# A two-layer convolution kernel: the filtered right-neighbour product in group one too, pair rounds between border batches, four stores from GpSimd

## The chip, the core and the metric

The kernel runs on one core of a Trainium2 chip. The core has TensorE (matmuls, into the accumulators `acc` in PSUM), VectorE, ScalarE, GpSimd and SyncE, each with its own instruction stream; they wait for each other by semaphores. Sixteen DMA engines move data to and from memory. The metric is the device time of one execution in microseconds (us), the median of several runs.

## The reference

Eight images of 32 channels and 64 x 64 pixels in float32. Two residual layers follow each other; `_gn` normalises each image and channel over its pixels.

```python
def _L0_conv_ref(x, w3, b3, w5, b5, wr, br):
    y3 = conv(x, w3) + b3            # 3 x 3, SAME
    y5 = conv(x, w5) + b5            # 5 x 5, SAME
    P = jnp.pad(y3, ((0, 0), (0, 0), (1, 1), (1, 1)))
    shifts = [P[:, :, 2 - sw:2 - sw + H, 2 - sh:2 - sh + W] for sh in range(3) for sw in range(3)]
    stacked = jnp.stack([y5] + shifts, axis=2)
    return jnp.einsum('bcghw,cg->bchw', stacked, wr[:, :, 0, 0]) + br[None, :, None, None]

def _L1_conv_ref(x, filters):        # filters: 32 x 32 x 10 x 10
    spot = _extract_patches(x, 3, 1, 1)                  # the 9 pixels around each pixel
    spot = jnp.concatenate([ones, spot], axis=-1)        # 1 and the 9 pixels
    feat = (spot[..., :, None] * spot[..., None, :]).reshape(spot.shape[:-1] + (M * M,))
    return jnp.einsum('bcyxf,ocf->boyx', feat, filters.reshape(O, C, M * M))

x = x + _L0_conv_ref(_gn(x), ...)
x = x + _L1_conv_ref(_gn(x), filters)
```

The second layer needs, for each channel, the pixels, their squares and the products of each pixel with its neighbours. The product of a pixel with its right neighbour is called NEXT in the kernel, the others have the numbers 7 to 17.

## The kernel before

**Tiling.** The images are worked on in two groups of four: group one (g = 0, images 0 to 3) and group two (g = 1, images 4 to 7). A group fills the 128 partitions, 32 channels by 4 images, in `raw[g]` (the input, later x after layer one) and in `plane[g]` (normalised, with borders). TensorE is used as a grid of 32 x 32 tiles: the row of the grid is the image r, the column the strip s. There are four strips of an image: s // 2 says which half of the rows, s % 2 which parity of rows. Even and odd pixel columns are summed apart, in `acc[:, 0]` and `acc[:, 1]` (j or `odd`).

**Rounds.** A filter column of three taps (`column`, L994 to L1023; layer one has the like in `column0`) is done in *pair rounds*, 8 matmuls with 64 columns of weights that serve two strips at once, and a *single round*, 16 matmuls with 32 columns of weights. Three rows of taps take two pair rounds and one single round. The order is an argument (`PS`, `SP`).

**Streams.** VectorE writes the products that TensorE reads as *streams*: a tile (`product[0..3]`, `raw0` or `raw1`, by `UNIT_HOME`) with an even and an odd half. `multiply` (L876) makes one product with 4096 elements a partition. The tiles are used in turn, so `wait_free` lets VectorE wait until TensorE has used what was there.

**Minimal filtering.** For the pixels themselves (linear) and their squares, even and odd columns are not filtered apart. VectorE makes sums and differences of neighbouring half-streams (`linear`, `of_product`: a sum, a cross, a left and a right one), and TensorE filters each with one set of three taps: `mixed_unit` for the sum and the cross, `side_unit` for left and right. The sum unit (j = 0) and the cross unit (j = 1) go to both outputs. ScalarE copies them out of `acc` (`keep_sum`, `keep_cross`), and VectorE adds them again in `mix` and `evict`. In group two the product NEXT is done in this way as well, with the shared taps `next_sum` and the sides `next left` and `next right`. In group one NEXT goes through `taps1`: two columns of taps for either parity.

**The order of the work.** It is written out by hand, engine by engine. TensorE: layer one of group one, layer one of group two, with the border batches of group one in it (`edges0`: matmuls of 64 pixels for the sides of the image), then for each group the shared units, the cross units, the sides, the products 7 to 17. The border batches of group two stand in the shared units of group one. Around them:

```python
keep_sum(0)            # ScalarE: waits for shared_done
spread(1, 0, (2,))
keep_cross(0)          # waits for the cross units
spread(1, 0, (3,))     # 4 copies
spread(1, 1, range(GROUP))   # 16 copies
```

`spread(g, odd, images)` copies layer one's result into `raw[g]`. On VectorE, `finish_x1(1)` (L817) waits for all these copies; behind it stand the statistics of group two, its normalisation, products 9 and 10, `mix(0)` and products 11 to 17:

```python
multiply(0, 7)
multiply(0, 8)
finish_x1(1)
step(statistics(1, lambda n: None, every))
normalise(3)
make_offset()
multiply(0, 9)
multiply(0, 10)
mix(0)
for u in range(11, LAST_UNIT + 1):
    multiply(0, u)
```

Layer one of group two on VectorE: `whole_and_cross(1)` (L663) needs TensorE's "step" part, then come `finish_x1(0)`, the statistics of group one's second layer, `normalise(2)` and `finish_even(1)` (L669), for which TensorE's first rounds of layer two wait.

**The end.** VectorE adds and writes the result in `evict` (L801), one image at a time. In group one SyncE stores all strips. In group two SyncE stores strips 0 and 1 and ScalarE strips 2 and 3: 16 stores of 128 KB, in rows of 256 bytes. SyncE waits for all of them.

Of the kernel before, what the change touches and what calls it, by code (L numbers as in the profile page):

```python
# [6 lines left out]
GROUP = 4  # L7
# [58 lines left out]
def n_taps(d):  # L66
# [11 lines left out]
UNIT_HOME = ({LINEAR: 1, SQUARE: 3, SQUARE_MIXED: 0, NEXT: 2, LINEAR_SIDES: "raw0", SQUARE_SIDES: 1,  # L78
              7: 3, 8: 0, 9: "raw0", 10: 1, 11: 2, 12: 3, 13: 0, 14: "raw0", 15: 1, 16: 2, 17: 3},
             {LINEAR: 0, SQUARE: "raw1", SQUARE_MIXED: 1, NEXT: 2, LINEAR_SIDES: 3, SQUARE_SIDES: 0, NEXT_SIDES: 1,  # L80
              7: "raw1", 8: 2, 9: 3, 10: 0, 11: 1, 12: "raw1", 13: 2, 14: 3, 15: 0, 16: 1, 17: "raw1"})


USED = ([LINEAR, SQUARE_MIXED, LINEAR_SIDES, SQUARE_SIDES, NEXT] + list(range(7, LAST_UNIT)),
# [3 lines left out]
MADE = (["square sum", "linear cross", "square cross", "linear left", "next", "square left", "linear right",  # L88
         "square right"] + list(range(7, LAST_UNIT + 1)),
# [9 lines left out]
def conv_kernel(nc, x, w3, b3, w5, b5, wr, br, filters, out):  # L99
# [12 lines left out]
    with ctx:  # L112
# [3 lines left out]
        def sem(name):  # L116
            return ctx.enter_context(nc.semaphore(name))
# [108 lines left out]
        stored = sem("stored")  # L226

# [76 lines left out]
        def store(eng, g, r, strips):  # L304

            for s in strips:
# [3 lines left out]
                              .rearrange("p (y x) -> p y x", x=W)).then_inc(stored, 16)  # L310
# [13 lines left out]
        def _(sp):  # L324
# [12 lines left out]
            for r in range(GROUP):  # L337
                sp.wait_ge(evicted, GROUP + r + 1)
                store(sp, 0, r, range(STRIPS))
            for r in range(GROUP):  # L340
                sp.wait_ge(evicted, 3 * GROUP + r + 1)
                store(sp, 1, r, (0, 1))
            sp.wait_ge(stored, 16 * NG * GROUP * STRIPS)

        @block.gpsimd
        def _(pool):
# [119 lines left out]
            stream_borders(raw[1]).then_inc(borders, 1)  # L466

        @block.scalar
        def _(act):
# [135 lines left out]
            for r in range(GROUP):  # L605
                act.wait_ge(evicted, 3 * GROUP + r + 1)
                store(act, 1, r, (2, 3))

        @block.vector
        def _(dve):  # L610
# [226 lines left out]
            def wait_free(g, u):  # L837

                if g == 0:
                    before = {SQUARE_SIDES: LINEAR, 8: SQUARE_MIXED, 9: LINEAR_SIDES, 10: SQUARE_SIDES, 11: NEXT,  # L840
                              12: 7, 13: 8, 14: 9, 15: 10, 16: 11, 17: 12}.get(u)
                    dve.wait_ge(borders, {3: 1, 0: 2, 1: 3, "raw0": 4, 2: 5}[UNIT_HOME[g][u]])
                elif u in (LINEAR, SQUARE_MIXED, NEXT, LINEAR_SIDES):
                    wait_used(dve, 0, {LINEAR: 13, SQUARE_MIXED: 15, NEXT: 16, LINEAR_SIDES: 17}[u])
                    before = None
                else:
                    before = {SQUARE_SIDES: LINEAR, NEXT_SIDES: SQUARE_MIXED, 8: LINEAR, 9: LINEAR_SIDES,
# [437 lines left out]
```

## Time and profile before

| | |
|---|---|
| median of 3 runs (lowest, highest) | 304.87 us (304.46, 305.16) |
| profiled execution, its own time | 305.6 us |
| its span, first to last instruction | 303.9 us |
| TensorE, weight loads, VectorE, ScalarE, GpSimd: busy share of the span | 91%, 41%, 83%, 29%, 11% |
| mean granted clock of TensorE | 0.979 |
| written to and read from memory | 4.19 and 6.40 MB |

The span is that of the profiled execution; 1.7 us of its own time lie around it. A busy share is a mean over the whole span. The timeline tells the start of a run of like instructions, its length, and in brackets how long the engine was idle before it and who released it; "issue" means that the profile shows nobody. The granted clock is 1.00 where TensorE runs at its upper level (2.4 GHz) and 0.50 at the lower (1.2 GHz). Each matmul of this kernel leaves two records and so does its weight load: 3232 matmuls, 6464 records.

### The profile page before, as it was taken

To read this page: it belongs to the slowest core of one execution; us is meant where nothing else is said; L and a number is where in the kernel's file an instruction comes from. 1 tells how busy PE (TensorE), PEld (TensorE's weight loads), DVE (VectorE), ACT (ScalarE), POOL (GpSimd) and SP (SyncE) were. 2 spreads that over 40 slices of the span, in tenths; PEclk is the share of its full clock that TensorE was granted. 3 is DMA by queue.
4 is the path that set the end of the run, shared out by engine and by line. 5 is a ranking of instruction groups with operands and counts; after the bars stand their busy time and mean duration, and the time that the engine had idled before them with its cause. 6 is when DMAs were issued, how large, how long until landed. Compare 5 with 4: busy or idle time off the path is not lost.

```text
span 303.9 us, 13566 instructions
## 1 busy us (share of the span) xinstructions
PE 276.0 (91%) x6464; PEld 125.6 (41%) x6464; DVE 251.5 (83%) x216; ACT 88.1 (29%) x135; POOL 33.0 (11%) x82
## 2 busy tenths in 40 slices
PE   0579999899999999999999999999999999999930
PEld 0124443343334434436457455333334446447310
DVE  1899899995999999599999999976999999950330
ACT  5432016949258989529000000004000000000000
POOL 7913970000110000000000000000000000000000
PEclk9999999979999999999999999999999999999985
DMA  6973000000000000000000000085000000000049
GB/s 191 382 193 82 4 3 2 2 5 2 2 2 4 4 2 2 4 2 5 2 2 4 4 2 4 2 172 111 2 2 4 2 2 4 2 4 4 2 86 190
DMA packets 19206, 11.45 MB, mean 38 GB/s; under 512 B 17744, under 2 KB 17872, under 8 KB 19024
## 3 DMA queue, kind: packets, MB, share of 16 engines
q1 hardware_dynamic: 14640, 9.06, 11.7%
q10 hardware_dynamic: 4512, 1.53, 2.2%
q8 instruction: 50, 0.82, 1.2%
q14 instruction: 4, 0.03, 0.0%
HBM read 6.40 MB, written 4.19 MB: 35 GB/s over the span
## 4 chain that ended last, share of the span: by engine, by line
PE 80%; DVE 7%; ACT 3%; issue 3%; DMA 2%; SPq 1%; DVEq 0%
PE acc L1007 63%; PE acc L1050 15%; ACT raw L507 3%; DMA raw<-in_x 2%; DVE stats L741 2%; PE acc L1101 2%; DVE plane L759 1%; DVE raw L801 1%; DVE arena L669 1%; ACT arena L497 1%; DVE scaled L637 0%; DVE norm L756 0%; SPq L314 0%; SPq L321 0%; DVE mean_var L746 0%
## 5 line engine op out<-in xcount | busy, mean ns | idle before, releaser
L1007 PE MATMUL acc<-product,weight 32*32 32x512 f32 (+1 forms) x3040 | 128.6, 605 | 0.0
L1007 PEld LDWEIGHTS acc<-product,weight 32*32 32x32 f32 (+1 forms) x3040 | 61.7, 110 | 63.8 <-issue 51.1
L879 DVE TENSOR_TENSOR product<-plane 128x4096 f32<-128x4096 f32 x19 | 83.3, 4427 | 0.1
L1007 PE MATMUL acc<-raw,weight 32*32 32x512 f32 (+1 forms) x992 | 44.3, 605 | 0.0
L1050 PE MATMUL acc<-product,middle 32*64 32x512 f32 (+1 forms) x576 | 30.6, 621 | 0.0
L1007 PEld LDWEIGHTS acc<-raw,weight 32*32 32x32 f32 (+1 forms) x992 | 20.4, 111 | 20.7 <-issue 16.2
L801 DVE TENSOR_TENSOR raw<-acc,arena 128x512 f32<-128x512 f32 x16 | 9.9, 684 | 18.9 <-issue 18.7
L741 DVE BATCH_NORM_STATS2 stats<-raw 128x6 f32<-128x512 f32 x32 | 19.7, 686 | 3.1 <-DMA raw<-in_x 3.1
L879 DVE TENSOR_TENSOR raw<-plane 128x4096 f32<-128x4096 f32 x5 | 22.2, 4433 | 0.0
L1007 PE MATMUL acc<-product,arena 32*32 32x512 f32 (+1 forms) x448 | 22.0, 606 | 0.0
L507 ACT ACTIVATE raw<-arena 32x512 f32<-32x512 f32 x32 | 21.9, 683 | 0.5
L537 ACT ACTIVATE arena<-acc 128x2048 f32<-128x2048 f32 x2 | 3.8, 1882 | 61.5 <-PE acc L1007 61.5
L507 ACT ACTIVATE raw<-product 32x512 f32<-32x512 f32 x28 | 19.2, 685 | 2.7 <-DVE product L669 2.3
L637 DVE TENSOR_TENSOR product<-plane 128x2048 f32<-128x2048 f32 (+1 forms) x8 | 18.5, 2324 | 0.0
L1050 PEld LDWEIGHTS acc<-product,middle 32*64 32x64 f32 (+1 forms) x576 | 11.0, 127 | 17.3 <-issue 17.1
L1120 PE MATMUL acc<-raw 32*64 32x512 f32 x64 | 5.7, 837 | 12.1 <-DMA raw<-in_x 11.0
L872 DVE TENSOR_TENSOR product<-product 128x2048 f32<-128x2048 f32 x6 | 13.6, 2289 | 0.6 <-PE acc L1007 0.6
L1007 PEld LDWEIGHTS acc<-product,arena 32*32 32x32 f32 (+1 forms) x448 | 7.5, 116 | 13.3 <-issue 12.5
L872 DVE TENSOR_TENSOR product<-raw 128x2048 f32<-128x2048 f32 x4 | 9.0, 2299 | 4.6 <-PE acc L1007 4.6
L860 DVE TENSOR_TENSOR product<-plane 128x2048 f32<-128x2048 f32 x5 | 11.3, 2297 | 0.0
L1050 PE MATMUL acc<-plane,weight 32*64 32x512 f32 (+1 forms) x192 | 10.4, 633 | 0.7 <-DVE plane L759 0.7
L1050 PE MATMUL acc<-product,minus_one 32*64 32x512 f32 (+1 forms) x192 | 10.8, 600 | 0.0
(121 smaller groups left out, 213.9 us busy)
## 6 DMA issues: line engine op xcount, KB each, us to landing
raw<-in_x SPq DMA_DIRECT2D x8, 512.0 KB, 8.5
out<-raw SPq DMA_DIRECT2D x24, 128.0 KB, 2.9
arena<-in_L_conv_filters SPq DMA_DIRECT2D x4, 400.0 KB, 6.9
out<-raw ACTq DMA_DIRECT2D x8, 128.0 KB, 4.6
arena<-in_L_conv_w ACTq DMA_DIRECT2D x4, 100.0 KB, 4.0
w_in<-in_L_conv_w ACTq DMA_DIRECT2D x2, 36.0 KB, 1.9
w_in<-in_L_conv_w SPq DMA_DIRECT2D x2, 36.0 KB, 2.1
b_in<-in_L_conv_b SPq DMA_DIRECT2D x2, 0.5 KB
```

The costliest lines, as they stand in the source:

```text
L507: last = nc.scalar.activation(to[:, y:y + SIDE_ROWS - 1:2, odd:odd + W - 1:2], half[32 * s:32 * s + 32, CHUNK * r:CHUNK * r + CHUNK] .rear ...
L537: nc.scalar.activation(kept_sum, part_acc(0), ACT.Copy).then_inc(shared_kept, 1)
L637: nc.vector.tensor_tensor(lines(buf, at, pitch)[:, 2:2 + H, 0:width], every_second(one), every_second(other), ALU.add if name == "total" e ...
L741: last = nc.vector.bn_stats(stats[:, n, :], raw[g][:, STAT * n:STAT * n + STAT])
L801: nc.vector.tensor_tensor(view(result, 2 * CHUNK * r + odd, (W, CHUNK // HALF_W), (2, HALF_W)), acc[:, odd, r, :].rearrange("p (y x) -> p ...
L860: nc.vector.tensor_tensor(half_stream(g, u, half), plane_half(g, one), plane_half(g, other), ALU.add if (sides, half) == (0, 0) else ALU.s ...
L872: nc.vector.tensor_tensor(half_stream(g, u, half), half_stream(g, source, *one), half_stream(g, source, *other), ALU.add if (sides, half) ...
L879: nc.vector.tensor_tensor(both_halves(g, u), plane_halves(g), plane_halves(g, PRODUCTS[k][0] * PITCH + PRODUCTS[k][1]), ALU.mult)\
L1007: return nc.tensor.matmul(acc[32 * s:32 * (s + strips), j, r, :], weights[32 * r:32 * r + 32, t:t + strips, :] .rearrange("p t c -> p (t c ...
L1050: return nc.tensor.matmul(acc[32 * s:32 * (s + strips), odd, r, :], five[32 * r:32 * r + 32, t:t + strips, :].rearrange("p t c -> p (t c)" ...
L1101: last = nc.tensor.matmul(acc[32 * s:32 * s + 32, 1, side, 0:W], weight0[32 * r:32 * r + 32, EDGE_AT + 5 * EDGE_PLACE[side] + t + 2, :], p ...
L1120: nc.tensor.matmul(acc[32 * s:32 * s + 64, 1, r, :], raw[0][32 * r:32 * r + 32, 0:64], raw[0][32 * r:32 * r + 32, 0:CHUNK], start=True, st ...
```

## The change

1. Group one computes NEXT by minimal filtering too. `next_unit` (three rounds) comes behind the square sum, ahead of the cross units, and `side_unit` does the left and the right side; the two columns of `taps1` fall away. VectorE makes NEXT as its second stream and adds `next left` and `next right`. The tiles of the streams are handed out anew, and group one's orders of pair and single rounds become those of group two; its products 7 to 17 begin with single rounds.
2. Between the two border batches of group one stand two pair rounds in the place of one single round; between those of group two four pair rounds in the place of two single ones, which go ahead of the first batch. Layer one's remaining parts of group two begin with single rounds.
3. In the 16 stores of group two strip 0 is SyncE's, strip 1 ScalarE's and strip 2 GpSimd's; strip 3 goes to ScalarE for images 0 and 2 and to SyncE for 1 and 3. GpSimd's four count on a semaphore of their own, for which SyncE waits last.

```diff
+USED = ([LINEAR, SQUARE_MIXED, LINEAR_SIDES, SQUARE_SIDES, NEXT_SIDES] + list(range(7, LAST_UNIT)),
+MADE = (["square sum", "next", "linear cross", "square cross", "linear left", "linear right", "square left",
+         "square right", "next left", "next right"] + list(range(7, LAST_UNIT + 1)),
...
+        def store_last(eng, strips, parity, done):
+
+            for r in range(GROUP):
+                eng.wait_ge(evicted, 3 * GROUP + r + 1)
+                store(eng, 1, r, strips + ((3,) if r % 2 == parity else ()), done)
...
-            for r in range(GROUP):
-                sp.wait_ge(evicted, 3 * GROUP + r + 1)
-                store(sp, 1, r, (0, 1))
-            sp.wait_ge(stored, 16 * NG * GROUP * STRIPS)
+            store_last(sp, (0,), 1, stored)
+            sp.wait_ge(stored, 16 * (NG * GROUP * STRIPS - GROUP))
+            sp.wait_ge(stored_by_pool, 16 * GROUP)
...
+            store_last(pool, (2,), None, stored_by_pool)
...
-            for r in range(GROUP):
-                act.wait_ge(evicted, 3 * GROUP + r + 1)
-                store(act, 1, r, (2, 3))
+            store_last(act, (1,), 0, stored)
...
             square_sum(0)
+            multiply(0, NEXT)
             linear_cross(0)
             square_cross(0)
             linear_left(0)
-            multiply(0, NEXT)
+            linear_right(0)
             square_left(0)
-            linear_right(0)
             square_right(0)
+            next_left(0)
+            next_right(0)
...
             edges0(0, ROW_SIDES)
-            product0(1, "total", 0, False, False, False)
+            product0(1, "total", 0, False, False, True, (-1, 0))
             edges0(0, COLUMN_SIDES)
-            product0(1, "total", 0, False, True, True).then_inc(part_done, 1)
+            product0(1, "total", 0, False, False, True, (1, 2))
+            product0(1, "total", 0, False, True, False).then_inc(part_done, 1)
             pe.wait_ge(edges_copied, 2)
-            rest0(1, PAIRS_FIRST)
+            rest0(1, SINGLES_FIRST)
...
+            def next_unit(g):
+
+                pe.wait_ge(stream_made, made(g, "next"))
+                column(0, stream_pixels(g, NEXT, 0), every_row, next_sum, False, False, PAIRS)
+                column(0, stream_pixels(g, NEXT, 0), every_row, next_sum, False, True, SINGLES)\
+                    .then_inc(shared_done, 1)
...
-                        column(0, plane_pixels(0, half), every_row, sum_taps[0][:, 0:3, :], half == 0, False, PAIRS)
+                        column(0, plane_pixels(0, half), every_row, sum_taps[0][:, 0:3, :], half == 0, False, SINGLES)
                     edges0(1, ROW_SIDES)
                     for half in (0, 1):
-                        column(0, plane_pixels(0, half), every_row, sum_taps[0][:, 0:3, :], False, False, SINGLES)
+                        column(0, plane_pixels(0, half), every_row, sum_taps[0][:, 0:3, :], False, False, PAIRS)
                     edges0(1, COLUMN_SIDES)
                     pe.wait_ge(borders, 5)
-                    mixed_unit(g, 0, "square", SP, stop=True).then_inc(shared_done, 1)
+                    mixed_unit(g, 0, "square", SP)
+                    next_unit(g)
...
-                side_unit(g, 0, "linear", SP if g else PS, start=True)
-                side_unit(g, 0, "square", PS if g else SP)
-                if g:
-                    side_unit(g, 0, "next", SP)
-                else:
-                    wait_made(g, NEXT)
-                    taps1(g, 0, NEXT, PAIRS)
-                    taps1(g, 0, NEXT, SINGLES)
+                side_unit(g, 0, "linear", SP, start=True)
+                side_unit(g, 0, "square", PS)
+                side_unit(g, 0, "next", SP)
                 pe.wait_ge(shared_kept, 2 * g + 2)
...
-                in_pairs = g == 0
+                in_pairs = False
```

TensorE at the first border place, in layer one of group two; rows of 32x64 (L1101) and 32x1 are a border batch, 64x512 are pair rounds (8 matmuls each), 32x512 single rounds (16). Before:

```order
16 L1050 MATMUL acc<-plane1,weight0 32x512 x16
17 L1101 MATMUL acc<-plane0,weight0 32x64 x40
18 L1109 MATMUL acc<-plane0,weight0 32x1 x16
19 L1050 MATMUL acc<-product3,middle0_1 32x512 x16
20 L1101 MATMUL acc<-plane0,weight0 32x64 x40
21 L1050 MATMUL acc<-product3,middle0_1 64x512 x64
22 L1050 MATMUL acc<-product3,middle0_1 32x512 x16
23 L1050 MATMUL acc<-product0,weight0 32x512 x16
```

The same place now:

```order
16 L1053 MATMUL acc<-plane1,weight0 32x512 x16
17 L1104 MATMUL acc<-plane0,weight0 32x64 x40
18 L1112 MATMUL acc<-plane0,weight0 32x1 x16
19 L1053 MATMUL acc<-product3,middle0_1 64x512 x16
20 L1104 MATMUL acc<-plane0,weight0 32x64 x40
21 L1053 MATMUL acc<-product3,middle0_1 64x512 x16
22 L1053 MATMUL acc<-product3,middle0_1 32x512 x32
23 L1053 MATMUL acc<-product3,middle0_1 64x512 x32
24 L1053 MATMUL acc<-product0,weight0 64x512 x32
```

Two pair rounds took the single round's place between the batches; behind the second batch follow two pair rounds, two single rounds and four pair rounds, where eight pair rounds and a single one ended the "step" part.

TensorE in layer two of group one, from the square sum (`product0`) to the cross units (reads of `product1` and `product0` with `arena` weights) and the first side. Before:

```order
36 L1007 MATMUL acc<-product0,arena 32x512 x16
37 L1007 MATMUL acc<-product0,arena 64x512 x16
38 L1007 MATMUL acc<-product1,arena 64x512 x16
39 L1007 MATMUL acc<-product1,arena 32x512 x16
40 L1007 MATMUL acc<-product0,arena 32x512 x16
41 L1007 MATMUL acc<-product0,arena 64x512 x16
42 L1007 MATMUL acc<-raw0,weight1 64x512 x16
```

Now:

```order
37 L1010 MATMUL acc<-product0,arena 32x512 x16
38 L1010 MATMUL acc<-product0,arena 64x512 x16
39 L1010 MATMUL acc<-product2,next_sum 64x512 x16
40 L1010 MATMUL acc<-product2,next_sum 32x512 x16
41 L1010 MATMUL acc<-product1,arena 32x512 x16
42 L1010 MATMUL acc<-product1,arena 64x512 x16
43 L1010 MATMUL acc<-product0,arena 64x512 x16
44 L1010 MATMUL acc<-product0,arena 32x512 x16
45 L1010 MATMUL acc<-raw0,weight1 32x512 x16
```

The `next_sum` rounds came in ahead of the cross units.

VectorE, from the first streams of group one to `finish_x1(1)` (L825); L872 are differences of half-streams, L860 linear ones, L879 whole products. Before:

```order
93 L860 TENSOR_TENSOR product1<-plane0 128x64x32
94 L872 TENSOR_TENSOR product0<-product3 128x64x32
95 L860 TENSOR_TENSOR raw0<-plane0 128x64x32
96 L879 TENSOR_TENSOR product2<-plane0 128x64x2x32
97 L872 TENSOR_TENSOR product1<-product3 128x64x32
98 L860 TENSOR_TENSOR raw0<-plane0 128x64x32
99 L872 TENSOR_TENSOR product1<-product3 128x64x32
100 L879 TENSOR_TENSOR product3<-plane0 128x64x2x32
101 L879 TENSOR_TENSOR product0<-plane0 128x64x2x32
102 L825 TENSOR_TENSOR edges<-edges,ring_corners 128x2x2
```

Now:

```order
93 L880 TENSOR_TENSOR product2<-plane0 128x64x2x32
94 L861 TENSOR_TENSOR product1<-plane0 128x64x32
95 L873 TENSOR_TENSOR product0<-product3 128x64x32
96 L861 TENSOR_TENSOR raw0<-plane0 128x64x32 x2
97 L873 TENSOR_TENSOR product1<-product3 128x64x32 x2
98 L873 TENSOR_TENSOR product0<-product2 128x64x32 x2
99 L880 TENSOR_TENSOR product3<-plane0 128x64x2x32
100 L880 TENSOR_TENSOR product2<-plane0 128x64x2x32
101 L830 TENSOR_TENSOR edges<-edges,ring_corners 128x2x2
```

NEXT (`product2`) moved ahead, and two half-stream differences of it (`product0<-product2`) are new ahead of `finish_x1(1)`.

## Rows read from the trace of the kernel before

**Rows 1.** The page: busy time, share of the span and instructions by engine.

```profile
PE 276.0 (91%) x6464; PEld 125.6 (41%) x6464; DVE 251.5 (83%) x216; ACT 88.1 (29%) x135; POOL 33.0 (11%) x82
```

**Rows 2.** The chain that ended last: start us, us, what.

```profile
101.03 185.72 PE acc L1007 x3955
```

**Rows 3.** VectorE's timeline: start us, us, what, count, idle before and releaser.

```profile
72.53 2.29 DVE L663 TENSOR_TENSOR arena<-arena,acc 128x2048 f32<-128x2048 f32 x1 [3.35 <-PE acc L1050]
...
107.22 2.29 DVE L872 TENSOR_TENSOR product<-product 128x2048 f32<-128x2048 f32 x1 [0.57 <-PE acc L1007]
...
126.16 0.17 DVE L825 TENSOR_TENSOR edges<-edges,ring_corners 128x4 f32<-128x4 f32 x1 [3.37 <-issue]
...
150.46 13.10 DVE L879 TENSOR_TENSOR product<-plane 128x4096 f32<-128x4096 f32 x3
...
199.06 4.49 DVE L860 TENSOR_TENSOR product<-plane 128x2048 f32<-128x2048 f32 x2
```

**Rows 4.** VectorE by stretch: from:to, length, busy (records), clock, DMA share, GB/s.

```profile
126.16:189.90 63.74, 62.88 (x46) 1.00 0.02 3
```

**Rows 5.** Timeline of TensorE's weight loads, group one's layer two.

```profile
106.68 0.55 PEld L1007 LDWEIGHTS acc<-product,arena 32*32 32x32 f32 x31 [0.35 <-issue]
108.07 0.23 PEld L1007 LDWEIGHTS acc<-product,arena 32*64 32x64 f32 x16 [0.84 <-issue]
...
159.27 6.27 PEld L1007 LDWEIGHTS acc<-product,weight 32*32 32x32 f32 x192 [0.18 <-DVE product L879]
...
168.33 0.29 PEld L1007 LDWEIGHTS acc<-raw,weight 32*32 32x32 f32 x32 [0.81 <-DVE raw L879]
```

**Rows 6.** TensorE by stretch: products 12 to 15, group one and group two.

```profile
159.27:176.94 17.67, 17.67 (x471) 1.00 0.01 4
254.85:272.50 17.65, 17.65 (x471) 1.00 0.01 4
```

**Rows 7.** ScalarE's timeline, layer one of group two and the `spread` copies.

```profile
67.66 1.88 ACT L497 ACTIVATE arena<-acc 128x2048 f32<-128x2048 f32 x1 [2.81 <-PE acc L1050]
...
110.19 1.88 ACT L544 ACTIVATE scaled<-acc 128x2048 f32<-128x2048 f32 x1 [1.24 <-PE acc L1007]
112.10 13.98 ACT L507 ACTIVATE raw<-arena 32x512 f32<-32x512 f32 x20
```

**Rows 8.** TensorE by stretch: group two, `next_sum` up to the first product.

```profile
201.78:228.66 26.88, 26.88 (x584) 1.00 0.25 54
```

**Rows 9.** TensorE's timeline, at both border places and at `next_sum`.

```profile
60.81 1.42 PE L1101 MATMUL acc<-plane,weight 32*32 32x64 f32 x75 [1.54 <-issue]
62.16 10.03 PE L1050 MATMUL acc<-product,middle 32*64 32x512 f32 x160
...
91.44 4.01 PE L1007 MATMUL acc<-plane,arena 32*64 32x512 f32 x64 [0.69 <-DVE arena L669]
...
99.88 1.02 PE L1101 MATMUL acc<-plane,weight 32*32 32x64 f32 x50 [0.38 <-issue]
...
201.78 3.13 PE L1007 MATMUL acc<-product,next_sum 32*64 32x512 f32 x64
204.55 6.29 PE L1007 MATMUL acc<-product,arena 32*32 32x512 f32 x128
```

**Rows 10.** DMA queue, kind: packets, MB, share; whole span, then 57.9 to 59.4.

```profile
q8 instruction: 50, 0.82, 1.2%
...
q8 instruction: 1, 0.02, 6.0%
```

**Rows 11.** All engines by stretch (PE, PEld, DVE, ACT, POOL), clock, DMA, GB/s.

```profile
62.40:65.70 3.30, 3.30 (x40) 1.18 (x32) 3.22 (x5) 2.36 (x8) 0.00 (x0) 0.50 0.00 0
```

**Rows 12.** SyncE's timeline: the stores of group one and of group two.

```profile
197.38 10.58 SPq L308 DMA_DIRECT2D out<-raw  x16
...
292.13 7.83 SPq L308 DMA_DIRECT2D out<-raw  x8
```

**Rows 13.** All engines by stretch, the end: clock, DMA share, GB/s come last.

```profile
293.10:303.10 10.00, 0.00 (x0) 0.00 (x0) 0.80 (x2) 0.00 (x0) 0.00 (x0) 0.57 1.06 208
```

More of the change, by code:

```diff
@@ L75 @@
 LAST_UNIT = N_PRODUCTS + 4
[L78 to L84, printed above, removed]
+UNIT_HOME = ({LINEAR: 1, SQUARE: 3, SQUARE_MIXED: 0, NEXT: 2, LINEAR_SIDES: "raw0", SQUARE_SIDES: 1, NEXT_SIDES: 0,
+              7: 3, 8: 2, 9: "raw0", 10: 1, 11: 0, 12: 3, 13: 2, 14: "raw0", 15: 1, 16: 0, 17: 3},
+             {LINEAR: 2, SQUARE: "raw1", SQUARE_MIXED: 1, NEXT: 0, LINEAR_SIDES: 3, SQUARE_SIDES: 2, NEXT_SIDES: 1,
+              7: "raw1", 8: 0, 9: 3, 10: 2, 11: 1, 12: "raw1", 13: 0, 14: 3, 15: 2, 16: 1, 17: "raw1"})
+USED = ([LINEAR, SQUARE_MIXED, LINEAR_SIDES, SQUARE_SIDES, NEXT_SIDES] + list(range(7, LAST_UNIT)),
         [LINEAR, SQUARE_MIXED, LINEAR_SIDES, SQUARE_SIDES, NEXT_SIDES] + list(range(7, LAST_UNIT)))
-MADE = (["square sum", "linear cross", "square cross", "linear left", "next", "square left", "linear right",
-         "square right"] + list(range(7, LAST_UNIT + 1)),
+MADE = (["square sum", "next", "linear cross", "square cross", "linear left", "linear right", "square left",
+         "square right", "next left", "next right"] + list(range(7, LAST_UNIT + 1)),
         ["linear sum", "linear cross", "square sum", "square cross", "next", "linear left", "linear right",
@@ L302, in made, with store @@
             return len(MADE[0]) * g + MADE[g].index(stream) + 1
-        def store(eng, g, r, strips):
+        def store(eng, g, r, strips, done):
             for s in strips:
@@ L1042, in plane_pixels, with column0 @@
                 return pixels
-            def column0(odd, stack, at, pitch, x0, every, five, start, stop, pairs):
+            def column0(odd, stack, at, pitch, x0, every, five, start, stop, pairs, rows):
                 def tile(r, s, strips, d, t, first_one, last_one):
@@ L1054, in column0 @@
                 if pairs:
-                    for d in range(-1, 3):
+                    for d in rows:
                         for s in (0, 2):
@@ L1064, in column0, with product0 @@
                 return last
-            def product0(g, name, odd, start, stop, pairs):
+            def product0(g, name, odd, start, stop, pairs, rows=range(-1, 3)):
                 if name == "next":
@@ L1070, in product0 @@
                     return column0(odd, plane[g], PLANE_AT - 2 * PITCH, PITCH, 2, 2, weight0[:, PAIR_AT:EDGE_AT, :],
-                                   start, stop, pairs)
+                                   start, stop, pairs, rows)
                 source, x0 = ("step", 1) if name == "step after" else (name, 0)
@@ L1077, in product0 @@
                 pe.wait_ge(middle_ready, g + 1)
-                return column0(odd, *half_at(g, source), x0, 1, five, start, stop, pairs)
+                return column0(odd, *half_at(g, source), x0, 1, five, start, stop, pairs, rows)
             def part(g, names, odd, forms):
```

34 lines of the change are left out of this document (12 added, 22 removed).

## The prediction, made before the result was known

> **What bounds the kernel now.** I read the share of busy time first and then, stretch by stretch, who waited for whom. TensorE is busy 91% of the span and VectorE 83% [rows 1], so a change that takes matmuls away must be read against VectorE's timeline too. The chain that ended last runs through TensorE for 186 us without a break, from 101.03 on [rows 2]. That looks as if every matmul removed from it were time saved. VectorE's timeline says otherwise. From 126.16 to 189.9 it is busy 62.88 us of 63.74 [rows 3, 4]. In that stretch it makes, among other work, the streams 9 to 17 of group one (images 0 to 3), a multiply of 4.34 us each: the three that begin at 150.46 (streams 11, 12, 13) are ready at 154.9, 159.2 and 163.6 [rows 3]. TensorE takes stream 12 the moment it is there: its first weights load at 159.27, released by the multiply, and so do those of stream 14 at 168.33 [rows 5]. From stream 12 on TensorE has a lead of 0.1 us or less, though it hardly waits yet: in group two, where VectorE is far ahead, the same 471 matmul records take 17.65 us, here 17.67 [rows 6]. **Two chains run level from 159 on.** A TensorE that is faster ahead of this place gains nothing there; a later VectorE costs in full.
>
> What sets VectorE's time? It stood idle for 3.37 us before `finish_x1(1)` at 126.16 [rows 3]. The view calls it "issue", but ScalarE's 20 copies of `spread` ran from 112.10 to 126.08 [rows 7], and `finish_x1(1)` waits for all of them. They stand in ScalarE's order behind `keep_cross(0)`, which began at 110.19 after a wait for TensorE [rows 7]. So the end is set by TensorE up to the end of group one's cross units (110.2), then ScalarE for 15.9 us, then VectorE for 33, then TensorE from stream 12 to the end. Call the moment at which `keep_cross(0)` begins K. The change is worth what it moves K, and what it does to the stores at the end.
>
> **Part 1: the filtered product in group one.** TensorE's work comes in rounds: 8 matmuls 64 columns wide or 16 of 32 (each matmul leaves two records). 27 rounds of group two take 26.88 us at the full clock [rows 8], 1.00 us a round. The right-neighbour product took 4 x 3 = 12 rounds in group one and takes 3 x 3 = 9 now, so TensorE is 3.0 us less busy. But of these nine, the shared three (`next_unit`) stand ahead of the cross units, where no round of this product stood. Group two has the same unit, from 201.78 to 204.55: **+2.8 us** on K [rows 9]. All the rounds that are saved lie behind K, where TensorE only runs further ahead: with what part 2 brings it would come to stream 11 some 3 us before it is made. The first product in the other order of forms costs at most one more turn from single to pair rounds, 0.5 us (1.4 for such a single round, from 106.68 to 108.07 [rows 5], instead of 0.9); the same wait hides it.
>
> VectorE gets two more half-stream subtractions (4.49 for two [rows 3]) and makes NEXT earlier. It was ready for `finish_x1(1)` at 122.8 (126.16 - 3.37). Plus 4.5, less the shift of part 2 (2.2), it comes at about 125.1, while ScalarE's copies end at 126.08 + 0.6 = 126.7. So these 4.5 us cost nothing under that cover, with 1.6 us to spare for waits longer than the 0.57 before 107.22 [rows 3]; without the cover they would cost all of 4.5. TensorE asks for NEXT at 91.44 - 2.2 + 9.2 (plane rounds and border batches) + 3.2 (square sum) = 101.6; VectorE has it at 97.8: no wait.
>
> **Part 2: pair rounds between the border batches.** In the first border place TensorE did a batch, one single round and the beginning of batch two, then nothing for 1.54 us, from 59.27 to 60.81 [rows 9]. No engine released it. What stands there is a packet of the instruction queue that begins between 57.9 and 59.4; 50 such packets carry 0.82 MB, one for 259 of TensorE's 12,928 records of matmuls and weight loads [rows 1, 10]. In the second border place there is a pause of 0.38 us before 99.88 [rows 9], behind a packet of the same kind that begins between 97.1 and 98.6. I read both as TensorE having used up its instructions: the small matmuls of a border batch go by at 75 records in 1.42 us even here [rows 9], those of a pair round at 16 in 0.9. Behind the first pause the clock fell to its lower level, 1.2 GHz: the stretch 62.4 to 65.7 has a granted clock of 0.50 [rows 11].
>
> Now two pair rounds (1.8 us, with as many records as the one single round of 0.9) stand ahead of batch two. The packet comes no sooner, so this batch ends at 62.16 as before, but the pause shrinks to 1.54 - 0.9 = 0.6 us. From 62.16 to the start of `whole_and_cross(1)` on VectorE (72.53, after a wait of 3.35 [rows 3]) it was 10.4 us. Now it is two pair rounds 1.8, two single ones 0.9 + 1.4, four pair rounds 3.5, drain 0.6: 8.2 us if the clock stays up, **-2.2 us**. VectorE is free from 69.2 on (72.53 - 3.35), so it can use that; ScalarE's `keep_whole(1)` (67.66, 1.88 us) begins at 65.3 then and its 12 copies of 0.70 end at 75.6 [rows 7], ahead of VectorE's 77. The chain behind it, up to `finish_even(1)` and TensorE's start at 91.44, moves along; TensorE waited 0.69 there [rows 9] and its own 25 rounds fit. If the clock falls all the same, 1.7 us of this are lost (3.4 us at half speed) and **-0.5** is left. I take -2.2: a pause of 0.6 is nearer to the 0.38 and the 0.69, behind which the clock stayed, than to 1.54.
>
> At the second border place single rounds now stand ahead of batch one, so I expect instructions to run short earlier, for about 1 us inside batch one; batch two then has four pair rounds ahead of it and no pause. Both together I put at 0 (-0.4 to +0.3; +1.7 if the clock falls there).
>
> The Trainium skill (Runtime: NRT & Kernel Launch, section Instruction fetch mechanics) holds that instructions come in 16 KiB blocks and that bringing them is hidden, since they are issued more slowly than they come. The pause of 1.54 us speaks against the second half; by that rule part 2 would move no pause, which is rival E below.
>
> **Part 3: the stores.** 16 stores leave at the end, 8 on each of two queues; SyncE's eight issues take 7.83 us [rows 12]. The DMA engines are full from 293.1 to 303.1: share 1.06, 208 GB/s [rows 13]. So what a third queue can save is the ramp of the first microsecond, 0.3 us at most. What it costs isn't in this trace, which has no DMA of GpSimd. SyncE's issues last 0.66 us each in group one (10.58 for 16) and 0.98 at the end [rows 12]; at either, GpSimd's four are out by 296.1 and cost nothing. The cost begins at (303.1 - 1.0 - 292.1) / 4 = 2.5 us a store, 1.0 being the time from the first issue to full engines. I take 0 and keep -0.3 to +3.
>
> The Trainium skill (DMA: Bandwidth & Descriptors, Specifications) gives about 1 us to the first byte for a DMA of GpSimd and 0.6 for the others; by that the sum grows by 0.4 us, and only if GpSimd's store lands last.
>
> **Sum.** K moves by 2.8 - 2.2 = +0.6, the lead at stream 12 takes up 0.1, the stores 0: **+0.5 us**. The profiled execution's 305.6 becomes 306.1, its span 303.9 becomes 304.4. The runs' median is 304.87, 0.7 below it, so 305.4.
>
> **The rivals.**
> A, a clock lost: as the forecast, but the clock falls at a border place or in the new waits. Ahead of stream 11 TensorE will be idle about 3 us and ahead of 12 another 2, more than the 1.54 that preceded a fall. Half speed for 3.4 us is 1.7 us of work; ahead of 12 the wait absorbs it, behind 12 nothing does. 305.4 + 1.7 = 307.1 (306.3 to 308.2). Chance 0.22.
> B, GpSimd's stores end last: 3.2 to 4 us each, so +2 to +5 with their landing, 307.4 to 310.4; it decides from 2.5 us a store. No row speaks for it, none excludes it. 0.11.
> C, faster by a little: the second border place gains its 0.4, VectorE starts at 69.2 rather than 70.4, the ramp gives 0.3: at best 305.4 - 1.9 = 303.5. 0.19.
> D, the rounds count in full, because streams come as early as TensorE asks for them: -2.2 - 3.0 + 0.5 = -4.7, so 300.2. For it: the chain names TensorE throughout [rows 2]. Against: loads released by a multiply and a lead of 0.1 us [rows 5]. 0.06.
> E, the pause is no want of instructions and stays, with the clock's fall: part 2 is worth 0, K moves by 2.8, 304.87 + 2.7 = 307.6. That is the skill's rule on fetching. For it: instructions were there at every other boundary. Against: both pauses stand behind a packet of that queue [rows 10]. 0.07.
> The forecast itself, 304.7 to 306.0: 0.35.
>
> **How the numbers follow.** 305.4 is the likeliest case. The range takes in C, the forecast, A, E and the near part of B: 303.4 to 308.0. D, the far part of B and the edge of A stay out, some 0.16. A measurement of this kernel tells 0.2%, 0.61 us, from no change: faster is below 304.26, slower above 305.48. Faster: D and most of C, 0.06 + 0.15. Same: the rest of C and 0.21 of the forecast's own range, 0.25. Slower: A, B, E and the forecast's upper part, 0.22 + 0.11 + 0.07 + 0.14 = 0.54.
>
> **What would show it.** ScalarE's copy behind the cross units begins 0.6 us later than 110.19. VectorE has no gap from `finish_x1(1)` to `evict(0, 0)`. TensorE is idle about 3 us ahead of stream 11 and 2 ahead of stream 12, with VectorE as releaser; that is where the saved rounds went. The granted clock stays whole from 62 to 66. The DMA engines are full from 293.7 to 303.6 and GpSimd's last issue begins before 299. I am wrong if TensorE has no such gaps and group two begins before 195, or if SyncE's last wait is for GpSimd's semaphore.

## The result, and the profile after

The changed kernel takes 309.06 us (306.58 to 309.72), the kernel before 304.85 in the same comparison: a ratio of 1.013 (95% interval 1.0083 to 1.0178), slower by 4.0 us. The forecast was 305.4 with a range up to 308.0, so it was wrong in size; slower was the likeliest sign. The profiled execution took 309.6 us, 4.0 more than the one of before, and its rows say where most of it lies.

The page of after, the busy times and GpSimd's queue, answers [rows 1] and [rows 10]:

```profile
PE 276.5 (90%) x6400; PEld 121.9 (40%) x6400; DVE 255.7 (83%) x218; ACT 87.8 (29%) x135; POOL 31.6 (10%) x86
...
q0 software_dynamic: 192, 0.52, 1.0%
```

64 matmul records are gone, and TensorE is no less busy. The chain that ended last (start us, us, what) is no longer TensorE alone from 101 on, as it was in [rows 2]:

```profile
151.84 2.03 DVE product L880
153.87 2.31 issue
156.18 4.42 DVE product L880
160.64 128.56 PE acc L1010 x2756
```

ScalarE's timeline, against [rows 7]; the copy of 1.88 us at 111.52 is `keep_cross(0)`, the moment called K:

```profile
66.36 1.88 ACT L504 ACTIVATE arena<-acc 128x2048 f32<-128x2048 f32 x1 [0.91 <-PE acc L1053]
...
111.52 1.88 ACT L551 ACTIVATE scaled<-acc 128x2048 f32<-128x2048 f32 x1 [1.30 <-PE acc L1010]
113.42 14.08 ACT L514 ACTIVATE raw<-arena 32x512 f32<-32x512 f32 x20
```

VectorE's timeline, against [rows 3]: `finish_x1(1)`, then the multiplies of streams 11, 12 and 13:

```profile
127.59 0.17 DVE L830 TENSOR_TENSOR edges<-edges,ring_corners 128x4 f32<-128x4 f32 x1 [1.34 <-issue]
...
151.84 13.09 DVE L880 TENSOR_TENSOR product<-plane 128x4096 f32<-128x4096 f32 x3
```

TensorE's timeline, against [rows 9] and [rows 5]: the first border place, streams 11 and 12, and group two's beginning:

```profile
61.43 1.42 PE L1104 MATMUL acc<-plane,weight 32*32 32x64 f32 x75 [0.40 <-issue]
...
156.31 3.32 PE L1010 MATMUL acc<-product,weight 32*32 32x512 f32 x64 [2.51 <-DVE product L880]
160.64 10.21 PE L1010 MATMUL acc<-product,weight 32*32 32x512 f32 x224 [1.01 <-DVE product L880]
...
198.18 6.28 PE L1010 MATMUL acc<-product,arena 32*64 32x512 f32 x128
```

All engines by stretch (granted clock, DMA share and GB/s come last); the first row answers [rows 11]:

```profile
62.40:65.70 3.30, 3.30 (x92) 1.27 (x75) 3.20 (x5) 2.44 (x8) 0.00 (x0) 1.00 0.03 5
157.20:164.00 6.80, 5.79 (x112) 1.79 (x96) 6.80 (x2) 0.00 (x0) 0.00 (x0) 0.50 0.02 5
```

And the end, against [rows 12]: the last stores as the three queues issue them.

```profile
294.59 6.37 SPq L309 DMA_DIRECT2D out<-raw  x6
294.60 6.48 ACTq L309 DMA_DIRECT2D out<-raw  x6
294.88 2.76 POOL L309 DMA_DIRECT2D out<-raw  x4 [157.28 <-DVE raw L806]
```

Read against the trace of before, they give three pieces. First, K is 1.3 us later (110.19 to 111.52). Of that 0.8 lies ahead of everything that the change touches: TensorE reached the first border batch 0.82 us later (57.51 after 56.69), 0.40 of it by a pause during layer one of group one. The other 0.5 is the forecast's 0.6. Second, the clock no longer falls behind the border place but behind the new waits, at 1.2 GHz for 6.8 us, and stream 13, before due 4.27 us behind stream 12 (159.36 to 163.63), now starts at 166.11, 5.47 behind it: 1.2 us lost. Third, the end: from the first issue to the end of the span it is 307.8 - 294.59 = 13.2 us, before 303.9 - 292.13 = 11.8. That makes 1.3 + 1.2 + 1.4 = 3.9 us, the difference of the spans.

### The profile page after: what moved, and what is told of

Read it like the earlier page. It is cut to its first block, busy times and chain, and to the rows that moved or that the text cites. A ratio compares the mean times of both kernels' runs of the same rounds, so it can differ in the third digit from the quotient of the medians.

```text
span 307.8 us, 13444 instructions
## 1 busy us (share of the span) xinstructions
PE 276.5 (90%) x6400; PEld 121.9 (40%) x6400; DVE 255.7 (83%) x218; ACT 87.8 (29%) x135; POOL 31.6 (10%) x86
## 4 chain that ended last, share of the span: by engine, by line
PE 73%; DVE 14%; ACT 3%; issue 3%; DMA 2%; SPq 1%; DVEq 0%; POOLq 0%; POOL 0%
PE acc L1010 56%; PE acc L1053 15%; DVE product L880 4%; ACT raw L514 3%; DVE stats L746 3%; DMA raw<-in_x 2%; PE acc L1104 2%; DVE plane L764 1%; DVE raw L880 1%; DVE raw L806 1%; DVE arena L789 1%; DVE arena L674 1%; ACT arena L504 1%; DVE arena L794 1%; DVE scaled L642 1%
## 5 line engine op out<-in xcount | busy, mean ns | idle before, releaser
L1010 PE MATMUL acc<-product,weight 32*32 32x512 f32 (+1 forms) x2912 | 125.8, 619 | 3.5 <-DVE product L880 3.5
L1010 PEld LDWEIGHTS acc<-product,weight 32*32 32x32 f32 (+1 forms) x2912 | 56.4, 111 | 70.2 <-issue 53.9
L309 POOL DMA_DIRECT2D out<-raw x4 | 2.8, 695 | 157.3 <-DVE raw L806 157.3
L873 DVE TENSOR_TENSOR product<-product 128x2048 f32<-128x2048 f32 x8 | 18.0, 2288 | 1.0 <-PE acc L1010 1.0
L1010 PEld LDWEIGHTS acc<-product,arena 32*32 32x32 f32 (+1 forms) x448 | 7.5, 116 | 13.2 <-issue 12.7
```

The costliest lines, as they stand in the source:

```text
L873: nc.vector.tensor_tensor(half_stream(g, u, half), half_stream(g, source, *one), half_stream(g, source, *other), ALU.add if (sides, half) ...
L1010: return nc.tensor.matmul(acc[32 * s:32 * (s + strips), j, r, :], weights[32 * r:32 * r + 32, t:t + strips, :] .rearrange("p t c -> p (t c ...
```

## The experiments

"Before" in these runs has a median of 304.7 to 304.85 us. Each ratio stands beside its 95% interval.

**The parts, one at a time.** Four kernels split the change: the new store code alone; everything but it; only the border pieces (`rows=`, SINGLES_FIRST and the two exchanged forms); only the filtered product.

```diff
 e1: +store_last(sp, (0,), 1, stored)  +store_last(act, (1,), 0, stored)
     +store_last(pool, (2,), None, stored_by_pool)
 e3: +product0(1, "total", 0, False, False, True, (-1, 0))
     +product0(1, "total", 0, False, False, True, (1, 2))
     +product0(1, "total", 0, False, True, False)
     (and PAIRS / SINGLES exchanged at the second border place)
 e4: UNIT_HOME, USED, MADE, next_unit(0), side_unit(0, ., "next", .)
 e2: e3 and e4
```

> The kernel before with the new store assignment alone. Theory S (the third queue costs by itself: in the changed kernel the last landing came 12.8 us after the first issue instead of 11.3): 304.9 + 1.4 = 306.3, and from the first store's issue to the end of the span 13.2 us instead of 11.7. Rival (the longer tail was chance or came from the rest of the change): 304.9, tail 11.7.

> The changed kernel with the stores of before. Theory (TensorE waits for VectorE ahead of products 11 and 12, and the clock falls in that wait; the stores cost 1.5 us on top): 309.1 - 1.5 = 307.6, waits of about 2.5 and 1 us ahead of products 11 and 12. If the clock falls late it costs 1.2 us behind them, if early nothing: single runs between 305.4 and 308. Rival (stores cost nothing): 309.

> The kernel before with the pair rounds between the border batches alone. Theory: the pause in the first border place shrinks from 1.5 to 0.4 us, the clock stays up, the copy behind the cross units begins 2 us earlier, VectorE reaches product 11 2 us earlier and TensorE takes over that gain: 304.9 - 2.0 = 302.9. Rival (the place was hidden, or the clock's fall was peculiar to the profiled run): 304.9.

> The kernel before with group one's filtered product alone (borders and stores of before). Theory (K moves by the three shared rounds, all saved rounds are lost in waits for VectorE): 304.9 + 2.8 = 307.7, plus up to 1.7 where the clock falls in the wait. Rival (the saved rounds count): 304.9 - 3.0 + 0.5 = 302.4.

Measured: stores alone 305.86 us, 1.0042 (1.0019 to 1.0065). All but the stores 307.81, 1.0097 (1.0064 to 1.0129). Borders alone 304.36, 1.0002 (0.9979 to 1.0026). Filter alone 308.03, 1.0111 (1.0080 to 1.0143). In microseconds: +1.3, +3.0, +0.1 and +3.4. The first two make 4.3, the whole change measured 4.0: the parts add up within their intervals.

The border pieces gain nothing, though they do what they were said to do. In their kernel TensorE's timeline has the short pause at the first border place, and the clock stays whole:

```profile
63.17 1.42 PE L1101 MATMUL acc<-plane,weight 32*32 32x64 f32 x75 [0.34 <-issue]
...
60.00:66.00 6.00, 5.66 (x211) 2.95 (x192) 5.86 (x10) 4.80 (x13) 0.00 (x0) 1.00 0.03 7
```

But the kernel before mostly keeps its clock there too, as far as its timed runs tell. Each comes with its mean granted clock, and the 77 runs of before fall into two heaps: 70 at 0.982 to 0.988, median 304.72 us, and 7 at 0.978 or 0.979, median 306.68. The one profiled execution on which the forecast rests, with 0.979, is of the second heap. (Where in those 7 runs the clock fell, no trace shows.) Four more kernels with the old border place show the pause with the clock whole: 0.84 us in e1, 1.02 in e4 and in e11, and 1.40 in e9, the kernel with twelve stores (below):

```profile
62.61 1.42 PE L1104 MATMUL acc<-plane,weight 32*32 32x64 f32 x75 [1.40 <-issue]
...
62.70:66.10 3.40, 3.40 (x115) 1.98 (x123) 3.29 (x6) 2.03 (x8) 0.00 (x0) 1.00 0.02 5
```

The kernel with `mix(0)` moved (e6, below) has nearly the same pause, and the clock falls; so it does in e10 (below), behind 1.35 us:

```profile
62.52 1.42 PE L1101 MATMUL acc<-plane,weight 32*32 32x64 f32 x75 [1.36 <-issue]
...
63.70:67.00 3.30, 3.30 (x44) 1.14 (x40) 3.21 (x6) 2.45 (x8) 0.00 (x0) 0.50 0.02 5
```

So at this place the length of the pause alone doesn't decide. From the first border batch to K it is 53.5 and 53.2 us in before and e6, in which the clock fell, 51.0 to 51.7 in the three unfiltered kernels with the old border place in which it didn't (e1, e9, e11), and 51.5 in e3. If all 7 low-clock runs of before fell at this place, the pair rounds save 2 us in 7 runs of 77, under 0.2 us in the mean.

The forecast's own step, from the end of the second batch to `whole_and_cross(1)`, can be read off as well (TensorE, then VectorE; e3, then e9):

```profile
64.53 7.87 PE L1050 MATMUL acc<-product,middle 32*64 32x512 f32 x152
73.11 2.29 DVE L663 TENSOR_TENSOR arena<-arena,acc 128x2048 f32<-128x2048 f32 x1 [1.55 <-PE acc L1050]
...
63.96 2.40 PE L1053 MATMUL acc<-product,middle 32*64 32x512 f32 x40
72.63 2.29 DVE L666 TENSOR_TENSOR arena<-arena,acc 128x2048 f32<-128x2048 f32 x1 [1.99 <-PE acc L1053]
```

That is 8.58 us with the pair rounds and 8.67 without them (8.67 in e1, e4 and e11 too, 8.3 to 8.8 in the other kernels with the pair rounds), all with the clock whole there; it is 10.37 in before and 10.24 in e6, behind a fall.

The filter's own trace has the waits, released by the multiplies, and the clock at half behind the first. ScalarE, TensorE, and all engines by stretch:

```profile
111.96 1.88 ACT L544 ACTIVATE scaled<-acc 128x2048 f32<-128x2048 f32 x1 [1.30 <-PE acc L1005]
...
156.73 3.63 PE L1005 MATMUL acc<-product,weight 32*32 32x512 f32 x64 [2.48 <-DVE product L875]
161.06 5.54 PE L1005 MATMUL acc<-product,weight 32*32 32x512 f32 x153 [0.70 <-DVE product L875]
...
156.40:159.80 3.40, 3.07 (x64) 1.03 (x64) 3.40 (x2) 0.00 (x0) 0.00 (x0) 0.50 0.02 5
```

From the first border batch to K it takes 53.75 us with the clock whole, against 51.0 to 51.7 without the filter: +2.0 to +2.7, near the price of the shared rounds, 2.8 [rows 9]. The clock fell in all 6 timed runs of this kernel and in 7 of 8 of e2, by the mean clock of each (0.974 to 0.981, below all of the 70 of before). What the fall costs depends on when it comes. In this trace it lasts from 156.4 to 159.8, and the wait for stream 12 takes it up: from K to the last piece of `evict` it is 182.7 us, not more than before (183.0, below). In the trace of e2 it comes behind the wait for stream 12, and there it is 184.1:

```profile
162.90:166.30 3.40, 3.40 (x78) 1.69 (x64) 3.40 (x1) 0.00 (x0) 0.00 (x0) 0.50 0.03 5
```

The account by K can be checked in every unfiltered profile in which ScalarE's order is the old one. From K to the start of the last piece of `evict` it is 183.03 us in the trace of before, and 183.0 to 183.1 in e1, e3, e6, e9 and e11, whose K ranges from 107.47 to 111.79. Whatever happened ahead of K moved the end one for one; nothing behind it did.

**Taking the waits away.** If TensorE's saved rounds are lost in waits for streams 11 and 12, an earlier stream must give them back. VectorE does the eight pieces of `mix(0)` (5.5 us, the rows between 146.41 and 151.84) ahead of product 11. `evict(0, 0)` alone needs them. e5 is e2 with `mix(0)` behind group one's last product; e6 is the kernel before with the same move.

```diff
-            mix(0)
             for u in range(11, LAST_UNIT + 1):
                 multiply(0, u)
+            mix(0)
```

> The changed kernel with the stores of before, and with mix(0) (5.5 us of VectorE) moved from ahead of product 11 to behind product 17. Theory (VectorE's supply binds at products 11 and 12): the waits of 2.5 and 1 to 2 us vanish, the clock stays up there, group one ends about 5 us earlier on TensorE and group two then waits for evict(0, 0), which VectorE reaches as late as ever: 307.8 - 4.5 = 303.3. Rival (the waits have another cause, or the 5.5 us are only moved and come back in full ahead of group two): 307.8.

> The kernel before with the same move of mix(0). Theory: before, TensorE had just enough lead (0.1 us) and lost nothing, so the move gains nothing: 304.7. Rival (VectorE held TensorE back before too): 302 to 303.

Measured: e5 304.22 us, 0.9981 (0.9956 to 1.0006), 3.6 us below e2. e6 304.67, 0.9991 (0.9967 to 1.0016): the move alone is worth nothing. The waits at streams 11 and 12 are gone; one of 2.1 us stands where `evict(0, 0)` now comes late, ahead of group two (VectorE, then TensorE):

```profile
190.55 2.48 DVE L801 TENSOR_TENSOR raw<-acc,arena 128x512 f32<-128x512 f32 x4
...
193.28 4.95 PE L1005 MATMUL acc<-product,arena 32*64 32x512 f32 x104 [2.06 <-DVE raw L801]
```

In this trace the clock stays whole until the end of the matmuls; two of the 12 timed runs (305.79 and 306.12 us) have a mean clock of 0.978 and 0.979, which speaks for a fall in them. VectorE has become the bound from K to 190, as K's chain says, and the next step is ScalarE, whose 20 copies held back `finish_x1(1)` by 1.36 us in this trace. e8 moves four of them ahead of the first copy out of `acc` and four ahead of the second, into time in which ScalarE waited for TensorE, so that 16 and not 20 stand behind K; e10 makes both moves in the kernel before, and e12 is e8 again, beside e10 on one chip.

```diff
+            spread(1, 0, (2,))
             keep_sum(0)
-            spread(1, 0, (2,))
+            spread(1, 0, (3,))
             keep_cross(0)
-            spread(1, 0, (3,))
             spread(1, 1, range(GROUP))
```

> As e5_mix_late, and ScalarE makes 8 of its copies of layer one ahead of the two copies out of the accumulators, where it sat idle, so that they no longer stand behind the cross units. Theory: finish_x1(1) on VectorE no longer waits (1.3 us), evict(0, 0) and group two come 1.3 us earlier than in e5_mix_late: 302.0. Rival (TensorE is the bound again in group one): no gain over 303.3.

> The kernel before (group one's right-neighbour product still direct) with the two moves of the best kernel so far: VectorE's mix(0) behind group one's last product, and ScalarE's spread(1,0,(2,)) and spread(1,0,(3,)) ahead of its two copies out of acc. It tells what the filtering of group one is worth once nobody waits for it. Theory 1 (the filtering removes 10 rounds net from layer two, about 9 us of matmuls, of which the three shared rounds ahead of cross units, 2.8 us, are added before the copies out of acc; with the waits gone its gain shows): this kernel lands at 304 to 305, 1.5 to 2 us above the filtered one with the same moves (302.85). Theory 2 (the filtering only moves time to VectorE, and the moves gained what was gained): this kernel lands at 302.5 to 303.5, within 0.7 us of it.

> The filtered kernel with both moves and the old stores once more, beside the unfiltered one with the same moves: 302.9 (302.3 to 303.5) by every theory; what is wanted is the difference of the two on one chip.

Measured: e8 302.85 us, 0.9918 (0.9888 to 0.9949). e12 302.39, 0.9926 (0.9903 to 0.9949). e10 305.3, 1.0019 (0.9994 to 1.0043). With both moves the filtered kernel beats the unfiltered one by 2.9 us (2 to 4 by the two intervals), and the kernel before by 2.3. e8 and e12 have the new border place too, and e10 the old one; no run has both moves with the filter alone. The traces set the border place aside: from the first border batch to the last piece of `evict` it is 232.3 and 232.6 us in e8 and e12, and 234.6 in e3, which has the new border place without the filter. The filter itself is then worth some 2 us. In e12 the copies end earlier, VectorE runs into `finish_x1(1)` without a gap, and TensorE waits 0.5 us (ScalarE, VectorE, TensorE):

```profile
111.14 1.88 ACT L544 ACTIVATE scaled<-acc 128x2048 f32<-128x2048 f32 x1 [1.30 <-PE acc L1005]
113.04 11.32 ACT L507 ACTIVATE raw<-arena 32x512 f32<-32x512 f32 x16
...
125.78 0.17 DVE L825 TENSOR_TENSOR edges<-edges,ring_corners 128x4 f32<-128x4 f32 x1
...
191.97 6.28 PE L1005 MATMUL acc<-product,arena 32*64 32x512 f32 x128 [0.51 <-DVE raw L801]
```

In e10 it is VectorE that waits for TensorE at that place: TensorE has more rounds to do, and an earlier stream helps nobody.

```profile
191.12 2.48 DVE L801 TENSOR_TENSOR raw<-acc,arena 128x512 f32<-128x512 f32 x4 [1.90 <-PE acc L1007]
```

**The stores.** e9 is e1 without GpSimd's four stores; strip 2 of images 4 to 7 is never written. e11 gives GpSimd one store (strip 2 of image 4) and the other three to SyncE and ScalarE.

```diff
 e9:  -            store_last(pool, (2,), None, stored_by_pool)
 e11: store_last(pool, ...) stops after r == 0; for r > 0 strip 2 goes to
      the queue that has no strip 3 in that turn (SyncE 7, ScalarE 8 stores)
```

> The kernel of e1_stores_only without GpSimd's four stores: strip 2 of images 4 to 7 is not written, SyncE and ScalarE make six stores each. Theory T1 (GpSimd's part slows the two other queues down, 12.8 us from the first issue to the last landing): without it 12 stores take 3/4 of the packets' time, 11.3 - 2.5 = 8.8 us. T2 (the new order of the stores on SyncE and ScalarE leaves the DMA engines short of work at the start): 10 us or more.

> The kernel before with the new store order, but GpSimd issues one of the last 16 stores (strip 2 of image 4), SyncE seven and ScalarE eight. Theory 1 (each 128 KB that GpSimd's queue carries delays the rest in proportion): first issue to last landing is 11.4 + 0.25 x 1.45 = 11.8 us, time 305.0. Theory 2 (the third queue's presence costs a fixed amount, whatever it carries): 12.6 to 12.9 us and 306. Theory 3 (it is only the order in which SyncE and ScalarE issue, not GpSimd): also 12.6 to 12.9, but with the full rate lost before GpSimd's first packet.

Measured: e9 303.13 us, 0.9946 (0.9918 to 0.9974). e11 305.5, 1.0012 (0.9991 to 1.0033). The timelines of the queues, e1 and then e11, have SyncE, ScalarE and GpSimd in this order:

```profile
289.41 6.32 SPq L309 DMA_DIRECT2D out<-raw  x6
289.41 6.43 ACTq L309 DMA_DIRECT2D out<-raw  x6
289.70 2.77 POOL L309 DMA_DIRECT2D out<-raw  x4 [156.22 <-DVE raw L806]
...
291.59 8.00 SPq L309 DMA_DIRECT2D out<-raw  x7
291.60 9.28 ACTq L309 DMA_DIRECT2D out<-raw  x8
291.88 0.83 POOL L309 DMA_DIRECT2D out<-raw  x1 [156.15 <-DVE raw L810]
```

The last landing, 0.4 us ahead of the end of each span, is 11.34 us behind the first issue in the trace of before (11.33 to 11.40 in all nine with the old stores), 11.76 in e11 with one store by GpSimd, 12.82 and 12.79 in e1 and after with four: 0.36 to 0.42 us for each store that moves to the third queue. A fixed cost of its presence above 0.42 us is excluded by e11. Most of the loss needs no GpSimd: by the sixteen of before, twelve stores should take 8.8 us (11.34 less a quarter of 10.1, the time in which 2.10 MB pass at 208 GB/s [rows 13]; an estimate), and e9's twelve take 9.7. That is 0.9 of the 1.45 us; the other 0.6 comes with GpSimd's four, which add 3.1 us where 2.5 were in proportion. All engines by stretch, the beginning and the last 2.8 us of the stores, after (with a stretch between), then e9, then before:

```profile
295.60:298.10 2.50, 0.00 (x0) 0.00 (x0) 0.76 (x2) 0.00 (x0) 2.04 (x4) 0.81 0.88 169
298.10:303.20 5.10, 0.00 (x0) 0.00 (x0) 0.00 (x0) 0.00 (x0) 0.00 (x0) 0.50 1.06 205
304.60:307.40 2.80, 0.00 (x0) 0.00 (x0) 0.00 (x0) 0.00 (x0) 0.00 (x0) 0.50 0.56 117
...
293.20:295.70 2.50, 0.00 (x0) 0.00 (x0) 0.77 (x2) 0.00 (x0) 0.00 (x0) 1.00 0.96 197
299.10:301.90 2.80, 0.00 (x0) 0.00 (x0) 0.00 (x0) 0.00 (x0) 0.00 (x0) 0.50 0.72 147
...
293.10:295.60 2.50, 0.00 (x0) 0.00 (x0) 0.80 (x2) 0.00 (x0) 0.00 (x0) 0.77 1.05 202
300.70:303.50 2.80, 0.00 (x0) 0.00 (x0) 0.00 (x0) 0.00 (x0) 0.00 (x0) 0.50 0.88 173
```

With six stores in each of SyncE's and ScalarE's queues the engines are filled to 0.88 (after) or 0.96 (e9) at first, not 1.05. In the last 2.8 us it is 0.72 without GpSimd's four and 0.56 with them, where before has 0.88 (and e11, with one, 0.80). With all three queues at work (from 298.1, when GpSimd's first packets begin, 3.3 us behind its first issue) they are full. The packets' own time is the same, 10.7 us on 16 engines: 31.6 + 28.9 + 23.2% of 12.8 us in after, 52.4 + 41.3% of 11.4 in before. So the engines stand idle for 12.8 - 10.7 = 2.1 us in after, 0.7 in before, and by the same working (80.6% of 9.7) 1.9 in e9. Why two queues with six stores each don't fill the engines where two with eight do is open; e9 shows only that GpSimd isn't needed for the larger part. e9 and the kernel before differ in two things, the number of stores and the order in which the strips go to the queues, and no run parts them.

## Why the prediction was wrong

**What held.** K as the moment that sets the end: the constant 183.0 us show it. The filter's three shared rounds on K: taken +2.8, seen +2.0 to +2.7 in e4; and from layer two's first matmul to K, 21.2 us there against 18.6 to 18.8 in the unfiltered kernels, 2.4 to 2.5 (2.5 to 3.2 in the five filtered kernels that have the new border place as well). The 4.5 us of subtractions on VectorE stayed under ScalarE's copies (1.34 left of the forecast's 1.6). TensorE's waits ahead of streams 11 and 12, forecast at 3 and 2 us, were 2.5 and 1.0. Rival D (the saved rounds count) was false as argued, because the streams weren't there.

**The step that failed first** is part 2's -2.2 us, measured as +0.1 (interval -0.6 to +0.8). The mechanism was right: the pause shrank from 1.54 to 0.40, the clock stayed up, `keep_whole(1)` began at 66.36 in place of 67.66. What was wrong was to set the sum against one profiled execution and then carry the difference over to a median. That execution's clock had fallen; the median's hadn't. 1.7 of the 2.2 us were the price of an event that 7 in 77 runs of before have: the forecast's 10.4 us from the second batch to `whole_and_cross(1)` are 8.67 wherever the clock is whole. The rest was a sum too small: the 8.2 us taken for the new order are 8.58 in e3, so that 0.1 us is left and not 0.5. The numbers of before could have raised the question: the profiled execution was 0.7 us above the median and above all three timed runs.

**The clock** was rival A, at a chance of 0.22; it should have been the likeliest case. Waits of 2.5 us for VectorE were followed by a fall in all three profiles that have them (after, e2, e4), and by the mean clock in 13 of the 14 timed runs of e2 and e4. The forecast argued that a fall ahead of stream 12 would be absorbed by its wait, and behind it by nothing. Both are so. The fall of e4's trace ends ahead of stream 12 and costs nothing. In after it lasts 6.8 us from 157.2 on, beyond the start of stream 12 at 160.64, and costs 1.2 us; in e2 it begins at 162.9, just behind stream 12's start at 162.26, and from K to the last piece of `evict` it is 1.1 us more than before. What the forecast had wrong is how often the clock falls there, and that it put nothing of it into the sum.

**The stores** were taken at 0 within -0.3 to +3; they cost 1.3 (0.6 to 2.0). The step "what a third queue can save is the ramp of 0.3 us, and its cost begins at 2.5 us a store" looked only at whether GpSimd's stores would land last. They landed 4 us ahead of the last (rival B is false) and the time was lost all the same: the larger part, 0.9 of 1.45 us, since the other two queues with six stores each didn't fill the engines. The Trainium skill (DMA: Bandwidth & Descriptors, section Issuing engines are not separate DMA queues) says that all issuing engines share the same 16 DMA engines and that a further one saves only its issue time. The runs agree that nothing is gained, and add that something is lost.

**The sum, again, against medians:** 304.7 + 3.4 for the filter (2.0 to 2.8 on K; that the rest is the clock is likely, not shown) + 0 for the borders + 1.3 for the stores = 309.4; measured 309.06. Rival E had part 2 at 0 for a false reason (it held that the pause stays) and came nearest with its 307.6.

The filter itself was a good change in the wrong surroundings: with the waits that it made taken away it is worth some 2 us, or 2.9 by the medians together with the new border place. What stays open: the size of the waits' clock loss run by run, since only one execution of each kernel has a trace, and whether the pair rounds between the border batches are worth anything in the best kernel (e12), where that wasn't tried.

## What to carry to other kernels

Before costing an edit against a profile, ask whether that execution is a typical one: compare its time and mean clock with the timed runs, and price a clock fall in it by how often it comes. Where two engines run level, fewer matmuls behind the meeting point give nothing until the other engine's order is changed too; find the moment whose distance to the end is constant (here K) and read every edit by that. A wait of 2.5 us on TensorE can cost more than it looks: in all three traces that have one the clock came down in it or soon after.

## What the runs showed of the hardware that was not expected

TensorE pauses with no engine to release it not only among border batches. It does so during layer one of group one too, while inputs still load, at the same instruction in each trace that has it. TensorE's timeline, the trace of e3:

```profile
28.29 7.38 PE L1050 MATMUL acc<-product,middle 32*64 32x512 f32 x131 [1.41 <-issue]
```

The same pause is 0.40 us in after, 0.39 in e4, 1.24 in e9, and absent in the nine others. It makes a part of the scatter between executions: the first border batch begins at 56.44 to 59.15 us, latest in e3, but without this pause too it is anywhere from 56.44 to 58.57. All pauses of TensorE of 0.24 us and more that no engine released behind the first 19 us stand, in all 13 traces, at position 192 modulo 256 among TensorE's instructions (matmuls, weight loads and semaphore waits counted). The Trainium skill (Runtime: NRT & Kernel Launch, section Instruction fetch mechanics) has blocks of 256 instructions and calls the crossing mostly hidden; the first agrees with the traces, the second doesn't hold for rounds of small matmuls here.

The queues' packets differ: GpSimd's 192 packets carry 0.52 MB, the 3168 of SyncE's 0.79 MB. In the stretch 294.6 to 307.4, the packets of GpSimd take 0.25 us each (23.2% of 12.8 us x 16 / 192) and SyncE's 0.020 (31.6%), which is 0.09 and 0.08 ns a byte:

```profile
q1 hardware_dynamic: 3168, 0.79, 31.6%
q10 hardware_dynamic: 3168, 0.79, 28.9%
q0 software_dynamic: 192, 0.52, 23.2%
```
